# A causal attention stage: weighted sums in pairs behind the scores, maxima in chunks, and four buffers of probabilities

## The reference, cut to what matters

```python
ql = x @ Wqd;  ckv = x @ Wkvd
q, qr = heads(ql @ Wqu), rope(heads(ql @ Wqr))
k, v  = heads(ckv @ Wku), heads(ckv @ Wvu);  kr = rope(x @ Wkr)
scores = (einsum('bhtd,bhsd->bhts', q, k) + einsum('bhtd,bsd->bhts', qr, kr)) * scale
scores = where(causal, scores, -inf)
out = einsum('bhts,bhsd->bhtd', softmax(scores), v) @ Wo
```

## Time and profile before

| | before |
|---|---|
| median of 3 runs | 2878.74 us |
| profiled execution | 2882.55 us |
| its span | 2880.8 us |
| TensorE (PE) busy | 2463.8 us, 86% |
| VectorE (DVE) busy | 1714.8 us, 60% |
| ScalarE (ACT) busy | 1346.1 us, 47% |
| GpSimd (POOL) busy | 1088.1 us, 38% |
| the main loop of the attention | 277 to 1103 us of the span |

### The profile page before, as it was taken

How to read it: one execution, slowest core, us unless ns; L and a number is a source line. 1 busy time by engine, 2 the same in 40 slices (tenths; PEclk the granted TensorE clock), 3 DMA queues, 4 the chain that set the end, 5 groups by cost and what they waited for, 6 DMA issues and landing times. The chain is left out here.

```text
span 2880.8 us, 44554 instructions
## 1 busy us (share of the span) xinstructions
PE 2463.8 (86%) x15815; PEld 1887.0 (66%) x15815; DVE 1714.8 (60%) x3579; ACT 1346.1 (47%) x2718; POOL 1088.1 (38%) x989
## 2 busy tenths in 40 slices
PE   4967888988988986796979989888968998898798
PEld 4855545544544544685867777677758887776687
DVE  7556754755745734655454997979835544545443
ACT  3424345344444444342226886768644444433232
POOL 2642101101102101452223663636446666757232
PEclk9987999999999996898989999999979999999899
DMA  4242000000000003223010000000033233323200
GB/s 160 80 123 67 16 9 15 19 16 9 18 9 14 5 1 108 69 82 109 30 38 8 1 1 8 1 8 1 8 110 89 83 90 94 98 83 99 88 1 30
DMA packets 77332, 136.58 MB, mean 47 GB/s; under 512 B 25792, under 2 KB 47256, under 8 KB 75968
## 3 DMA queue, kind: packets, MB, share of 16 engines
q0 software_dynamic: 26336, 73.01, 8.5%
q1 hardware_dynamic: 50784, 60.72, 6.6%
HBM read 112.48 MB, written 20.81 MB: 46 GB/s over the span
## 5 line engine op out<-in xcount | busy, mean ns | idle before, releaser
L1442 ACT ACTIVATE PT<-ps 128x512 f32<-128x512 f32 (+3 forms) x640 | 302.9, 535 | 416.4 <-PE ps L1199 415.9
L2304 POOL DMA_INDIRECT KV<-kv_scratch,sidx x384 | 369.2, 962 | 213.9 <-issue 132.8
L35 PE MATMUL ps<-KIh,qih 128*128 128x512 f32 (+2 forms) x640 | 247.8, 387 | 50.5 <-DVE Isc L1888 40.8
L1319 DVE TENSOR_REDUCE xn<-ps 128x1 f32<-128x512 f32 x384 | 238.2, 682 | 70.7 <-PE ps L1184 70.7
L1948 POOL TENSOR_TENSOR part_sum<-part_sum,rlp 128x1024 f32<-128x1024 f32 (+7 forms) x120 | 210.6, 1755 | 86.6 <-ACT rlp L1774 85.4
L36 PE MATMUL ps<-KIl,qih 128*128 128x512 f32 (+2 forms) x640 | 239.4, 374 | 0.0
L1888 DVE SCALAR_TENSOR_TENSOR Isc<-ps,iw,Isc 128x1024 f32<-128x1024 f32 (+7 forms) x216 | 208.6, 966 | 51.7 <-ACT ps L1798 46.1
L37 PE MATMUL ps<-KIh,qil 128*128 128x512 f32 (+2 forms) x640 | 238.5, 373 | 0.0
L1798 ACT ACTIVATE ps<-ps,iwa 128x1024 f32<-128x1024 f32 (+7 forms) x240 | 198.2, 858 | 47.3 <-PE ps L37 46.6
L2226 ACT ACTIVATE sP<-sP,snm 128x128 f32<-128x128 f32 (+2 forms) x256 | 110.4, 432 | 232.5 <-DVE snm L2289 229.4
L35 PEld LDWEIGHTS ps<-KIh,qih 128*128 128x128 f32 x640 | 123.6, 193 | 96.0 <-issue 74.6
(11 more groups left out here) (356 smaller groups left out, 6763.1 us busy)
## 6 DMA issues: line engine op xcount, KB each, us to landing
cs<-in_rope SPq DMA_DIRECT2D x20, 512.0 KB, 4.1
ycomb<-y_rows SPq DMA_DIRECT2D x16, 512.0 KB, 4.9
w1raw<-in_w SPq DMA_DIRECT2D x14, 512.0 KB, 6.7
KV<-kv_scratch,sidx POOLq DMA_INDIRECT x384
xn_rows<-xnr SPq DMA_DIRECT2D x8, 512.0 KB, 4.9
w2raw<-in_w SPq DMA_DIRECT2D x14, 256.0 KB, 7.0
wir<-in_wi SPq DMA_DIRECT2D x1, 2176.0 KB, 7.8
X<-in_x SPq DMA_DIRECT2D x1, 2048.0 KB, 8.3
```

Source lines behind the costliest of these rows:

```text
L35: pe.matmul(out, lhs[0], rhs[0], start=start, stop=False)
L1319: v.tensor_reduce(mp[:, row, s:s + 1], o, AX_X, ALU.max).then_inc(a_free, 1)
L1442: s.activation(PT[:, rnd % 2, hh, lo:CH], ps[:, BANK[kind, u, j, r, hh % 2], lo:CH], ACT.Exp, scale=SCALE).then_inc(a_exp, 1)
L2304: g.indirect_dma_start(KV[:, BG * (k % RB) + m, :], None, a["kv_scratch"], bass.IndirectOffsetOnAxis(sidx[:, t % 2, at:at + 1], 0)).then_i ...
```

## The change

There are three parts.

1. attend(u) visits the sums at every second key tile. For an odd j the order is S(j-1) twice, S(j) twice, and then A(j-3) and A(j-2); before, A(j-1) stood between the two steps of S(j). The last two sums of a unit follow the first two key tiles of the next one. What stood between key tiles (L, D, V, G, O, F, N, W) follows behind each such pair (new function between); E follows the scores of tile 2.
2. PT has PTR = 4 buffers instead of 2, and the exponentials of a round wait for the sum four rounds back.
3. A step M holds one chunk of keys instead of all c+1 (new function maxima), so that blend can put other steps between the chunks. Its price in pe_us is that of one chunk.

```diff
-        PT = sb("PT", [P, 2, GH, CH], F32, a_ctx)
+        PTR = 4
+        PT = sb("PT", [P, PTR, GH, CH], F32, a_ctx)
...
+        def maxima(c):
+
+            yield from ((s,) for s in range(c))
+            yield (c,)
...
-                order += [("M", u, p, r) for r in range(CT)]
+                order += [("M", u, p, (r, chunks)) for r in range(CT) for chunks in maxima(u % NCH)]
...
         def attend(u):
 
+            for j in range(CT * (u % NCH + 1)):
+                yield "S", u, j, 0
+                yield "S", u, j, 1
+                if j == 2 and u >= 1:
+                    yield "E", u - 1, 0, 0
+                if j % 2 == 0:
+                    continue
+                if j >= 2:
+                    yield "A", u, j - 3, 0
+                    yield "A", u, j - 2, 0
+                elif u >= 1:
+                    yield "A", u - 1, CT * ((u - 1) % NCH + 1) - 2, 0
+                    yield "A", u - 1, CT * ((u - 1) % NCH + 1) - 1, 0
+                yield from between(u, j - 1)
+                yield from between(u, j)
+
+        def between(u, j):
+
             g, c = u // NCH, u % NCH
-            for j in range(CT * (c + 1)):
-                yield "S", u, j, 0
-                if j >= 1:
-                    yield "A", u, j - 1, 0
-                elif u >= 1:
-                    yield "A", u - 1, CT * ((u - 1) % NCH + 1) - 1, 0
-                yield "S", u, j, 1
-                if j == 0 and u >= 1:
-                    yield "L", u - 1, 0, 0
-                    yield "D", u - 1, 0, 0
...
-                if j == 1 + (c >= 1) and u >= 1:
-                    yield "E", u - 1, 0, 0
...
+            if j == 0 and u >= 1:
+                yield "L", u - 1, 0, 0
+                yield "D", u - 1, 0, 0
...
         def pe_us(step):
             if step[0] == "M":
-                return 0.47 * (step[1] % NCH + 1) + 0.08
+                return 0.47 * len(step[3][1]) + 0.02
...
                 begin = two.index(("S", u, CT * 2, 0)) if u % NCH == NCH - 1 else 0
                 yield from blend(prepare(u + 1) if u + 1 < NU else [], two, begin)
+            yield "A", NU - 1, CT * NCH - 2, 0
...
                         if hh == 0:
-                            s.wait_ge(a_av, max(rnd - 1, 0))
-                        s.activation(PT[:, rnd % 2, hh, lo:CH], ps[:, BANK[kind, u, j, r, hh % 2], lo:CH], ACT.Exp, scale=SCALE).then_inc(a_exp, 1)
+                            s.wait_ge(a_av, max(rnd - PTR + 1, 0))
+                        s.activation(PT[:, rnd % PTR, hh, lo:CH], ps[:, BANK[kind, u, j, r, hh % 2], lo:CH], ACT.Exp, scale=SCALE).then_inc(a_exp, 1)
```

More of the change, by code:

```diff
@@ new lines, in between @@
+        def between(u, j):
+            g, c = u // NCH, u % NCH
+            if j == 0 and u >= 1:
+                yield "L", u - 1, 0, 0
+                yield "D", u - 1, 0, 0
+                if c == 0:
+                    yield "V", g, 1, 0
+            if j == 1 and c == 1 and g >= 1:
+                yield "G", u - 2, 0, 0
+                yield "O", g, 0, 0
+            if j == 2 + (c >= 1) and u >= 1:
+                yield "F", u - 1, 0, 0
+            if j == 3 + (c >= 1) and u >= 1:
+                yield "N", u - 1, 0, 0
+            if j == 6 and c >= 1:
+                yield "G", u - 1, 0, 0
+            if c == NCH - 1 and g + 1 < NG:
+                if j < NP:
+                    yield "W", g + 1, j, 0
+                if j == CT * 2 + 1:
+                    yield "V", g + 1, 0, 0
@@ L1082, in build @@
         for kind_, u_, h_, r_ in STEPS:
-            for k_ in range({"K": 2, "P": 3, "M": 2 * (u_ % NCH + 1), "R": 1, "F": 1, "G": 2, "S": 2}.get(kind_, 0)):
+            for k_ in range({"K": 2, "P": 3, "M": 2 * len(r_[1]) if kind_ == "M" else 0, "R": 1, "F": 1, "G": 2, "S": 2}.get(kind_, 0)):
                 key_, bank_ = (kind_, u_, h_, r_, k_), RING[turn % len(RING)]
@@ L1171, in attn_tensor @@
                 elif kind == "M":
-                    p, tok = h, slice(r * P, (r + 1) * P)
+                    p, (row, chunks) = h, r
+                    tok = slice(row * P, (row + 1) * P)
                     pe.wait_ge(a_qhi, NP * u + p + 1)
@@ L1176, in attn_tensor @@
                         pe.wait_ge(a_kb, u + 1)
-                    for s in range(c + 1):
-                        wide = CH if s < c else max(2 * P, (r + 1) * P)
+                    for at, s in enumerate(chunks):
+                        wide = CH if s < c else max(2 * P, (row + 1) * P)
                         keys = slice(CH * s, CH * s + wide)
-                        o = [take(kind, u, p, r, 2 * s + k) for k in range(2)]
+                        o = [take(kind, u, p, r, 2 * at + k) for k in range(2)]
                         for k, own in enumerate(HALVES):
@@ L1211, in attn_tensor @@
                     for hh in range(GH):
-                        i = pe.matmul(ps[2 * HD * hh:2 * HD * (hh + 1), AV_BANK, lo:CH], VG[:, j, hh, :], PT[:, ROUND[u, j] % 2, hh, lo:CH],
+                        i = pe.matmul(ps[2 * HD * hh:2 * HD * (hh + 1), AV_BANK, lo:CH], VG[:, j, hh, :], PT[:, ROUND[u, j] % PTR, hh, lo:CH],
                                       start=j == 0, stop=j == last_key(u))
@@ L1313, in attn_vector @@
                 elif kind == "M":
[L1314 to L1324, removed]
+                    at, (s,) = r
+                    for k in range(2):
+                        o = full(kind, u, h, r, k)
+                        part = mp[:, CT * (NP * k + h) + at, s:s + 1]
+                        if s < c:
+                            v.tensor_reduce(part, o, AX_X, ALU.max).then_inc(a_free, 1)
+                        else:
+                            end = (at + 1) * P
+                            seen = cm_bf[:].rearrange("p a t -> p (a t)")[:, CH - end:CH]
+                            v.tensor_tensor_reduce(out=o[:, 0:end], in0=o[:, 0:end], in1=seen, scale=1.0, scalar=LEAST,
+                                                   op0=ALU.add, op1=ALU.max, accum_out=part).then_inc(a_free, 1)
                 elif kind == "X":
-                    v.wait_ge(a_free, PIECE["M", u, NP - 1, CT - 1, 2 * c + 1] + 1)
+                    v.wait_ge(a_free, PIECE["M", u, NP - 1, (CT - 1, (c,)), 1] + 1)
                     if u >= 1:
@@ L1478, in attn_gpsimd @@
                     rnd = ROUND[u, h]
-                    own = PT[:, rnd % 2, :, st_start(u, h):st_start(u, h) + P]
+                    own = PT[:, rnd % PTR, :, st_start(u, h):st_start(u, h) + P]
                     p.wait_ge(a_exp, GH * (rnd + 1))
```

16 lines of the change are left out of this document (removed).

## The result

The changed kernel takes 2810.60 us (median of 4 runs, 2804.72 to 2812.11) against 2877.56 us (4 runs, 2873.49 to 2880.06): ratio 0.9765, 95% interval 0.9746 to 0.9783, that is 67 us faster. The prediction said 2800 (2778 to 2830), a gain of 79 us. The profiled execution took 2810.73 us, span 2808.7, so the two profiled executions differ by 71.8 us; times inside the trace, which follow, belong to this larger figure.

What follows compares the result with a forecast made beforehand. TensorE was taken to bound the attention loop; gains of 26.1 (chunk 3), 10.3 (last unit), 32 (chunk 2), 6.8 (chunk 1) and 4 (chunk 0) sum to 79 us, from 2878.74 to 2800 us, range 2778 to 2830.

Steps and rivals of the forecast that it cites:

- The bound and the waits of sums: Main attention loop: TensorE sets the pace; sums stop waiting for exponentials (30.5 us) and the accumulator copy (9.7 us).
- chunk 3: Three units of the loop: 65.5 us each falls to 56.8, gain 8.7 each, 26.1 in all.
- the last unit: Final unit of the loop, which prepares nothing: 47.7 against 58.0 us, gain 10.3.
- The price of a change and of a neighbouring sum: TensorE: 0.135 us per change of array shape, 463 changes become 337; a sum directly behind a sum takes 0.93 us.
- SyncE's queue keeps D, E and R in the same order: DMAs in the loop: same number, only shifted within the unit; in chunk 3 F is met with about 1 us to spare.
- I add 4.5 us for this coupling: Chunk 2: 4.5 us added for TensorE and VectorE not both meeting their floors, so 56.2 us, gain 8.0 each.
- two floors: Chunk 2: TensorE's own time 51.1 us and VectorE's floor 51.7 us; rival that both are met: 2779 us, 14%.
- The wait of the first scores for QN: Start of a unit after chunk 2: R to S has 2.5 us against 3.2 needed, 0.6 us inside VectorE's floor.
- The split of the gain: Chunk 2: gain 8.0 us each, of which 4.5 if only the waits of sums and of F go while VectorE's remain.
- Chunk 1: Four units of the loop, VectorE already the bound: gain 1.7 us each, 6.8 in all, ends 0 and 3.
- Chunk 0: Four units of the loop: net gain 1.0 us each, 4 in all, ends -1.0 and 2.5.
- The clock rival: Loop: longer pieces of pure maxima lower TensorE's clock; at mean 0.86 it costs 98 us, kernel at 2898 us; 3%.

Runs made afterwards that it cites:

- late single sums: Kernel before with A(j-2) singly between the two steps of S(j), three buffers, maxima unsplit: 2847.69 us, ratio 0.9914 to the kernel before.
- single chunks alone: Kernel before with only the maxima in single chunks, old attend and PTR = 2: 2835.05 us, ratio 0.9858 to the kernel before.
- pairs alone: Kernel before with sums in pairs and four buffers, a row's maxima still in one step: 2815.65 us, ratio 0.9801 to the kernel before.
- the halved kernel before: Kernel before with maxima of chunks before the diagonal read over 256 of 512 columns: chunk 2 64.25 to 57.7 us (single execution).
- the version by chunk: Changed kernel with single late sums in chunks 0 to 2, pairs in chunk 3, W later: 2966.77 us, ratio 0.9721 to the kernel before.
- W later: Changed kernel with head weights W at key tiles 4 and 5 instead of 0 and 1: units 3, 7, 11 take 56.96, 57.03, 56.95 us.

## Why the prediction was right, and where its steps were not

*The bound and the waits of sums: right.* TensorE sets the pace of the loop, and the waits of sums for exponentials and for the accumulator copy went, in chunk 3 and in the last unit as written. Those 34.5 us (22.6 + 11.9) have their cause shown twice: late single sums alone give 4.5 us in a unit of chunk 3 and 6.8 in the last, pairs the rest, while single chunks alone leave both where they were (65.3 and 58.0). In the last unit the 5.2 us between late single sums and pairs are not changes alone: 20 changes at 0.17 are 3.4 us, and late single sums keep a wait of 0.8 us for the accumulator copy and one of 0.7 us before the last sum.

*The price of a change and of a neighbouring sum: too small and too large.* The pair in unit 11 of the changed kernel:

```profile
800.08 0.40 PE L1216 MATMUL ps<-QN,XTh 64*128 64x512 f32 x2
800.41 1.92 PE L1229 MATMUL ps<-PT,VG 128*32 128x512 f32 x16
802.26 0.70 PE L1235 MATMUL ps<-xn,spread 128*128 128x512 f32 x1
```

Two wide sums take 1.85 us, where one takes 1.00. The second costs 0.85, not 0.93. So the stream of a sum is 0.85, and of the 1.66 us around an isolated one 0.345 are the two changes, 0.17 each; late single sums against pairs gave 0.15 to 0.19. The Trainium skill ("TensorEngine Tiling (Array Packing)", Key Properties) says that TensorE is drained by a change of the tiling mode and not by one of the tile; these rows, 0.85 against 1.00 us, agree.

In most units the two errors nearly cancel: in chunk 2 the streams are 0.9 us less and 28 changes 1.0 us more, and the sum stays 51.1. In the last unit they take 1.3 us off and put 0.6 on. The other 0.9 of the 1.6 us by which it beat the forecast (46.1 for 47.7) is a slip of adding: at the prediction's own prices the matmuls of this unit come to 43.5 us before and 43.9 after, where it had 44.4 and 44.9.

*"SyncE's queue keeps D, E and R in the same order": the step that failed in chunk 3.* It does, but W's four weight DMAs stand between D and E. In the kernel before, they were issued in two halves, and E's DMA of unit 3 left 0.9 us after its reciprocal's end, behind the second half, with time to spare before F; with L, D, W and W together and F four steps S behind, the four issues (3.3 us in unit 3) put F 2.0 and 0.9 us late. Unit 11 has no W on that queue and took 56.97 against my 56.8. 3 us of the missing 3.5 are this.

*"I add 4.5 us for this coupling": too little in chunk 2.* 57.65 came for 56.2. From the first M to X the unit takes 46.0 us with VectorE busy for 40.1, where the prediction had 39 of some 43. The 4.5 was a guess between two floors, and 3.6 us or more still go with VectorE's work. The wait of the first scores for QN came as written (0.6 us).

The split of the gain was near the mark in one half: 4.5 us were forecast if only the waits of sums and of F went, and pairs alone gave 4.7. (The expectation for the halved kernel before reads that 4.5 as VectorE's share; it was the share of the others, so VectorE had some 8 of the 12.6 us of stall, against 6.5 or more measured.) What the prediction lacked is that the finer maxima take most of the same time: alone they give 7.0 us, more than the 6.6 of the whole change. TensorE's waits in unit 10 show it. Before:

```profile
PE ps L1199 <- DVE xn L1319: 2.9, 5, 0.7
PE ps L1212 <- ACT PT L1442: 2.1, 3, 1.3
PE ps L1218 <- DMA xn<-xn: 1.2, 1, 1.2
PE ps L1182 <- DVE xn L1319: 0.5, 1, 0.5
```

with single chunks alone (here L1219 is the sums, L1206 the scores, L1189 the maxima):

```profile
PE ps L1219 <- ACT PT L1449: 1.0, 2, 0.6
PE ps L1206 <- DVE xn L1326: 0.4, 1, 0.4
PE ps L1189 <- DVE xn L1326: 0.3, 1, 0.3
```

with pairs alone (L1215 is the scores):

```profile
PE ps L1215 <- DVE xn L1336: 3.2, 6, 0.7
```

and with the whole change:

```profile
PE ps L1216 <- DVE xn L1336: 0.7, 2, 0.5
PE ps L1216 <- DMA QN<-xn: 0.6, 1, 0.6
PE ps L1216 <- DVE xn L1340: 0.5, 1, 0.5
```

Single chunks take away most of the waits for VectorE, all of F's and half of the sums', since chunks between an S and its A give the exponentials time. Why VectorE then holds TensorE up less is argued: a step of eight banks on a ring of seven must wait for reductions of its own. No run isolates it, and it can't be all, since in chunk 1, whose steps of three chunks take six banks, single chunks alone gave 1.8 us of 45.0.

Once single chunks are there, late single sums win 1.15 us more (56.1), and pairs lose 0.4 (57.65 against 57.3; in chunk 1 43.8 against 43.2). TensorE's order in unit 10 has stretches of three steps S without any maxima with pairs, where single sums leave one or two. That this is the reason is argued from the order, not isolated; that keeping the pairs together costs more (58.1) fits it. So the total of chunk 2 came near the forecast partly by luck: the guess of 4.5 covered an overlap of the two parts that the prediction had not seen.

*Chunk 1: right in size, for the reason given.* VectorE is the bound; 1.7 us came, single chunks alone gave 1.8 and pairs alone 0.3, and halving VectorE's reductions gave 3.7 more. *Chunk 0: right within its spread.*

*The clock rival: it did not come.* 0.99 over the loop. In chunk 0 the clock did fall in some units. Unit 4 and unit 8 of the changed kernel run the same order:

```profile
465.54:498.99 33.45, 28.24 (x184) 15.78 (x183) 24.11 (x61) 12.20 (x27) 7.63 (x8) 0.90 0.10 28
658.38:690.36 31.98, 25.65 (x185) 14.79 (x185) 24.11 (x61) 12.20 (x27) 7.63 (x8) 1.00 0.07 19
```

At 0.90 the unit takes 1.5 us more than at 1.00, with VectorE's work equal. Much of the spread of chunk 0 goes with the clock (the unit of 34.8 us in the version by chunk ran at 0.85), but its mean doesn't fix the price: with late single sums and single chunks units 8 and 12 take 31.55 us at 1.00 and 31.50 at 0.95.

Of the 12 us between the forecast gain of 79 and the 67 of the medians, 6.5 lie in the units of the trace (79 to 72.6: 5.7 too much in chunk 2 and 3.5 in chunk 3, 2.5 too little elsewhere). The other 5.5 lie between traces and medians: the profiled execution before took 2882.55 us against a median of 2877.56, the one after 2810.73 against 2810.60, stages outside the loop took 0.8 us back, and the prediction took the difference within the trace for that of the medians.

## What to carry to other kernels

Two edits that each take away a wait can take away the same one: run each alone before giving either the gain, since 40 and 59 us alone made 67 together here. Where a second engine is near its bound, feed it small pieces steadily and keep the first engine's long runs for the stretches in which the second has nothing to do; the order by chunk was worth some 10 us over one order for all stretches (13.5 less 3 for W later). When steps are gathered at one point, list every queue they issue on: the new waits here were a DMA behind four others and exponentials behind a copy that waited for its DMA.

## What the runs showed of the hardware

A second group of matmuls in the same shape of the array costs its stream alone: 0.85 us against 1.00 for one on its own up to the next start and 1.20 with both changes. And four DMA issues on SyncE's queue took 2.0 us in unit 7 but 3.3 in unit 3, so the same issues can take a different time at the same place of the program; why, stays open.
